# A quantised feed-forward is rebuilt with the weights in the expert loop, work by quarters and written-out pairs

## The chip, the core and the metric

The kernel runs on one core of a Trainium2 chip. A core has TensorE (PE in the profile), VectorE (DVE), ScalarE (ACT), GpSimd (POOL) and SyncE (SP), which only issues DMAs here. Each engine works through its own list of instructions in order, and the engines meet at semaphores. The metric is the time of one execution on the device in microseconds (us); smaller is better.

## The reference, cut to what matters

Two layers run on `x` of 16 x 256 tokens with 128 features. The first is relative-position attention and a mixture of 8 experts. The second is linear attention and a feed-forward whose operands are rounded to 4-bit floating point by blocks of 16. The change is about this last part:

```python
def fp4_quant_dequant(x):                      # blocks of 16 along the last dimension
    scale = jnp.maximum(jnp.max(jnp.abs(xb), axis=-1, keepdims=True) / 6.0, 1e-12)
    idx = jnp.searchsorted(_MID, jnp.abs(xb / scale))
    return _GRID[idx] * jnp.sign(xb / scale) * scale      # grid 0 .5 1 1.5 2 3 4 6
def fp4_linear(x, w):
    return einsum('bsk,nk->bsn', fp4_quant_dequant(x), fp4_quant_dequant(w))
h = layernorm(x) * (1 + cb) + sb
gate, up = fp4_linear(h, w_gate), fp4_linear(h, w_up)     # 352 hidden features
x = x + gb * fp4_linear(silu(gate) * up, w_down)
```

## The kernel before

The 4096 tokens are 32 tiles of 128 tokens (one token a partition). Four tiles are a chunk, eight tiles a quarter, two tiles a pair. `R2` holds the residual stream of all tiles.

**Expert loop** (about 556 to 831 us). Eight chunks `tc`, in each 16 half experts `k`. TensorE makes two products (`experts_up`, L1125 to L1127), ACT takes silu into `SG`, DVE multiplies (`hidden_product`, `hb_done`), ACT and DVE or POOL split the result into two half-precision parts (`low_hidden`, L608 on POOL), and TensorE makes the down product (`expert_down`), which DVE adds up (`weigh`). TensorE waits for the product two halves back (`hb_done`). Functions called `beside(tc, k)` put small pieces of other work at chosen places of this loop on each engine: the gating, and for some chunks statistics and normalisation of the next layer. Pieces are Python generators that give one instruction or a few at each `next`.

**Linear attention** (831 to 933 us). Its last step is eight output projections (L1233), each followed by a multiplication with the gate on DVE (`gate_projection`, L1528, semaphore `l_mul`) and an addition to `R2` on POOL (`residual`, L518, `l_od`).

**Preparation of the feed-forward** (933 to 998 us). DVE takes the statistics of the norm in two halves (L1306 to L1316). POOL clears `FN` (L637), SP loads the three weight matrices into it, POOL makes the inverse roots (`inverse_root`, L493), ACT centres the 32 tiles (`centre`, L712). DVE quantises the weights in two parts (L1779 to L1785, L1796; 768 and 352 columns), TensorE turns them (L1242, L1247), DVE copies them out of PSUM (L1800 to L1802). DVE scales the eight chunks (`scaled`, L1323), POOL adds the shift (`shifted`, L502). Then the input is quantised in four quarters, each 128x1024: seven DVE instructions (`quantise`), namely

```python
step(nc.vector.tensor_reduce(am[0], x, AX_X, ALU.max, apply_absolute_value=True))   # L1779
step(TS(am[2], am[0], ...))                # L1780, block scale
step(nc.vector.reciprocal(am[1], am[2]))   # L1781
step(STT(m, x, 2.0 ** -23 - 1.0, inv, ALU.mult, ALU.mult))                          # L1782
step(TS(s.bitcast(I32), m.bitcast(I32), ...))                                       # L1783
step(STT(m, s, 1.5 * 2 ** 22, m, ALU.max, ALU.add))                                 # L1784
return STT(m, s, 1.5 * 2 ** 22, m, ALU.max, ALU.subtract), scale                    # L1785
```

and on POOL the multiplication with the block scale (L644, into `XQ`). `step` waits for each instruction before the next. TensorE turns `XQ` (L959), ACT copies it to `R1` (L878).

**Pair loop** (998 to 1142 us). 16 pairs `m`, rolled in hardware loops (`Fori`) of two pairs on every engine:

- TensorE: `gate_and_up(m+1)` (L1261, 4 products of 352 columns from the stationary operand `XT`), then `hidden_and_down(m)`: six transposes of the quantised hidden `HQ` (L1270) and, after ACT's copy, six down products (L1277).
- ACT: `silu_gate` (L893, `SGP`, one buffer, 128x704), `evacuate_hidden` (L899, L900, `HT`, one buffer), `stationary` (L883, from `R1` to `XT`), `evacuate_output` (L889, `YB`).
- DVE, `hidden(m)`: the product `SGP` x up, up read from PSUM (L1825, `f_h`), and the seven steps of `quantise` on 128x704. The next gate product waits for `f_h`, since the up result lies in the bank that it writes.
- POOL: `scale_hidden` (L661, `f_q`), and `output`: multiplication with the gate (L651) and addition to `R2` (L655).
- SP: after every second pair 8 DMAs of finished tiles (L464).

Of the kernel before, what the change touches and what calls it, by code (L numbers as in the profile page):

```python
# [5 lines left out]

# [74 lines left out]
def adaln_program(nc, a, out):  # L81
# [17 lines left out]
    with outer:  # L99
# [74 lines left out]

        l1 = ExitStack()
# [18 lines left out]
        FN = sb("FN", [128, 6 * 128 + FF], F32, ff)  # L194
        WGU = sb("WGU", [128, 2, FF], F32, ff)
        WD1 = sb("WD1", [128, 3, 128], F32, ff)

        SGP = sb("SGP", [128, 2, FF], F32, ff)
        HQ = [sb(f"HQ{j}", [128, 2, FF], F32, ff) for j in range(2)]
        XT = [sb(f"XT{j}", [128, 2, 128], F32, ff) for j in range(2)]  # L200
        HT = sb("HT", [128, 2, 3, 128], F32, ff)
# [42 lines left out]
        f_ye, f_yg, x_round = sem("f_ye"), sem("f_yg"), sem("x_round")  # L244
# [36 lines left out]
        def _(sp):  # L281
# [170 lines left out]
            sp.wait_ge(l_od, 8)  # L452
# [8 lines left out]
            with sp.Fori(0, NT // 4) as c:  # L461
                sp.wait_ge(f_out, 2 * c + 2)
                for l in range(IL):
                    sp.dma_start(out_tok[l][:, bass.ds(4 * c, 4), :],  # L464
                                 R2[B * l:B * (l + 1), bass.ds(4 * c, 4), :]).then_inc(stored, 16)
# [4 lines left out]
        def _(gp):  # L470
# [17 lines left out]

            def inverse_root(n):
                for half in range(2):  # L490
                    tiles = slice(NT // 2 * half, NT // 2 * (half + 1))
                    gp.wait_ge(var_ready, 17 + half)
                    gp.tensor_tensor(LN[:, 2, tiles], LN[:, 1, tiles], LN[:, 5, tiles], ALU.pow).then_inc(root_done, 1)  # L493
                    gp.wait_ge(root_done, 17 + half)
                    gp.tensor_tensor(LN[:, 3, tiles], LN[:, 0, tiles], LN[:, 2, tiles], ALU.mult).then_inc(rstd_ready, 1)

            def shifted(order, dst, shift, ready):

                for c in range(8):
                    gp.wait_ge(scale_done, c + 1)  # L500
                    t = dst[:, 4 * c:4 * c + 4, :]
                    gp.tensor_tensor(t, t, shift.unsqueeze(1).to_broadcast([128, 4, D]), ALU.add).then_inc(ready, 1)  # L502
# [65 lines left out]
            for h in range(H - 1):  # L568
                sums_to_dram(h)
                normalise(h)  # L570
            for q in range(4):
# [63 lines left out]
            residual(l_mul, R2, [CT[j][:, :] for j in range(2)], l_od)  # L635
            gp.wait_ge(l_od, 8)
            gp.memset(FN[:, :], 0.0).then_inc(zeroed, 1)  # L637
            inverse_root(5)
            shifted(3, HN3, MOD[1][:, 3, :], pre_ready)
            BLOCKS = NT * D // 16 // 4  # L640
            for c in range(4):
                k = slice(BLOCKS * c, BLOCKS * (c + 1))
                gp.wait_ge(x_round, c + 1)
# [4 lines left out]
            def output(m, v):  # L648

                gp.wait_ge(f_ye, m + 2)  # L650
                gp.tensor_tensor(YB[v][:, :, :], YB[v][:, :, :], MOD[1][:, 5, :].unsqueeze(1).to_broadcast([128, 2, D]), ALU.mult)\  # L651
                    .then_inc(f_yg, 1)
                gp.wait_ge(f_yg, m + 1)
                x = R2[:, bass.ds(2 * m, 2), :]
                gp.tensor_tensor(x, x, YB[v][:, :, :], ALU.add).then_inc(f_out, 1)  # L655

            def scale_hidden(m, v):

                gp.wait_ge(f_round, m + 1)
# [3 lines left out]

            gp.sem_inc(f_q, 1)
            scale_hidden(0, 0)
            with gp.Fori(0, PAIRS // 2 - 1) as c:
                for v in range(2):
                    scale_hidden(2 * c + v + 1, 1 - v)
                    output(2 * c + v, v)
            scale_hidden(PAIRS - 1, 1)  # L670
            output(PAIRS - 2, 0)
            output(PAIRS - 1, 1)


        @block.scalar
        def _(act):
# [29 lines left out]

            def centre(k, src, dst, done, before=0):

                for n in range(NT):
                    if n % (NT // 2) == 0:  # L710
                        act.wait_ge(rstd_ready, 17 + n // (NT // 2))
                    last = A(dst[:, n, :], src[:, n, :], ACT.Identity, bias=LN[:, 3, n:n + 1], scale=LN[:, 2, n:n + 1])  # L712
                    if n % 4 == 3:
                        last.then_inc(done, 1)
# [94 lines left out]

            def high_hidden(tc, k):  # L810
# [62 lines left out]
            centre(5, R2, HN3, centred)  # L873

            def evacuate_x(chunks):
                for c in chunks:
                    act.wait_ge(t_done, 24 + c + 1)
                    A(R1[:, 512 * c:512 * c + 512], banks[4 + c % 2][:, :], ACT.Copy).then_inc(t_evac, 1)  # L878

            evacuate_x(range(6))  # L880

            def stationary(m, v):
                A(XT[v][:, :, :], R1[:, bass.ds(256 * m, 256)].rearrange("p (u t) -> p u t", u=2), ACT.Copy).then_inc(f_xt, 1)  # L883

            def evacuate_output(m, v):
                act.wait_ge(f_y, m + 2)
                if not (isinstance(m, int) and m < 2):
                    act.wait_ge(f_out, m - 1)
                A(YB[v][:, :, :], PS[:, 6:8, 0:128], ACT.Copy).then_inc(f_ye, 1)  # L889

            def silu_gate(m):
                act.wait_ge(f_gu, m + 1)
                A(SGP[:, :, :], gate_up[:, :, 0], ACT.Silu).then_inc(f_sg, 1)  # L893

            def evacuate_hidden(m):
                act.wait_ge(f_ht, m + 2)
                act.wait_ge(f_y, m + 1)
                t = PS[:, 4:6, 0:384].rearrange("p u (c t) -> p u c t", c=3)
                A(HT[:, :, 0:2, :], t[:, :, 0:2], ACT.Copy)  # L899
                A(HT[0:96, :, 2, :], t[0:96, :, 2], ACT.Copy).then_inc(f_hv, 1)  # L900

            act.sem_inc(f_hv, 1)
            act.sem_inc(f_ye, 1)
            act.wait_ge(t_evac, 30)
            stationary(0, 0)
            stationary(1, 1)
            silu_gate(0)
            evacuate_x(range(6, 8))
            act.wait_ge(t_evac, 32)
            stationary(2, 0)  # L910
            silu_gate(1)
            evacuate_hidden(0)
            stationary(3, 1)
            evacuate_output(0, 0)
            silu_gate(2)
            evacuate_hidden(1)
            stationary(4, 0)
            evacuate_output(1, 1)
            with act.Fori(1, PAIRS // 2 - 2) as c:
                for v in range(2):  # L920
                    silu_gate(2 * c + v + 1)
                    evacuate_hidden(2 * c + v)
                    stationary(2 * c + v + 3, 1 - v)
                    evacuate_output(2 * c + v, v)
            for m in range(PAIRS - 4, PAIRS):
                if m + 1 < PAIRS:
                    silu_gate(m + 1)
                evacuate_hidden(m)
                if m + 3 < PAIRS:
                    stationary(m + 3, (m + 1) % 2)  # L930
                evacuate_output(m, m % 2)
# [3 lines left out]
        def _(pe):  # L935
# [16 lines left out]
            def transposes(k, src, chunks=range(8)):  # L952

                for c in chunks:
                    pe.wait_ge(h_ready, 8 * k + c + 1)
                    if c >= 2:
                        pe.wait_ge(t_evac, 8 * k + c - 1)
                    for j in range(4):
                        last = tr(banks[4 + c % 2][:, 128 * j:128 * j + 128], src[:, 4 * c + j, :], ident)  # L959
                    last.then_inc(t_done, 1)  # L960
# [11 lines left out]
            for q in range(4):  # L972
                transposes(0, HN, (2 * q, 2 * q + 1))
# [128 lines left out]
            def linear_transposes(c):  # L1102
# [4 lines left out]
                elif c >= 2:  # L1107
                    pe.wait_ge(t_evac, 16 + c - 1)
                for j in range(4):
                    last = tr(banks[6 + c % 2][:, 128 * j:128 * j + 128], HN2[:, 4 * c + j, :], ident)  # L1110
                last.then_inc(t_done, 1)

# [34 lines left out]
            def beside(tc, k):  # L1147
# [90 lines left out]
            pe.wait_ge(f_w, 1)  # L1238
            for w in range(2):
                for c in range(3):  # L1240
                    m = (128, 128, 96)[c]
                    last = tr(banks[w][:, 128 * c:128 * c + m], FN[0:m, 384 * w + 128 * c:384 * w + 128 * c + 128],  # L1242
                              ident[0:m, 0:m])
            last.then_inc(f_tr, 1)
# [616 lines left out]
```

## Time and profile before

| | |
|---|---|
| time, median of 3 runs (lowest to highest) | 1143.52 us (1142.25 to 1144.01) |
| time of the profiled execution | 1143.78 us |
| span of its trace, first to last instruction | 1142.0 us |
| busy: TensorE, DVE, ACT, POOL | 884.3, 734.3, 453.7, 411.9 us |
| mean granted TensorE clock | 0.878 of full speed |
| first hidden maximum in the pair loop starts | 998.89 us |
| last instruction of the last rounding ends | 1127.10 us |

The device time is a little longer than the span of the trace. A granted clock of 1.00 is 2.4 GHz for TensorE and 0.50 is 1.2 GHz; a value between them is a mean over a stretch. Names with a "q" (SPq, POOLq) are an engine's queue of DMA issues. In a row, `out<-in` names the tiles, and what stands in square brackets is the idle time of the engine before the instruction and what ended it.

### The profile page before, as it was taken

What the parts mean: (1) busy time and instruction counts of PE and PEld (TensorE: products, weight loads), DVE (VectorE), ACT (ScalarE), POOL (GpSimd) and SP (SyncE); (2) the same over time, 40 slices, a digit from 0 to 9 for tenths busy, and PEclk for the clock granted to TensorE, in tenths of its full rate; (3) what the DMA queues carried; (4) which work ended last, traced back from release to release, by engine and by line L of the source; (5) the groups of instructions that cost most, each with busy time, mean ns of one, the idle gap of its engine ahead of it and who ended that gap; (6) DMA issues with size and microseconds to landing.
All of it is one profiled execution on the core that took longest, in us unless ns stands there. A gap on an engine that the chain in (4) does not pass through costs nothing.

```text
span 1142.0 us, 22164 instructions
## 1 busy us (share of the span) xinstructions
PE 884.3 (77%) x8587; PEld 671.1 (59%) x8587; DVE 734.3 (64%) x1571; ACT 453.7 (40%) x748; POOL 411.9 (36%) x447
## 2 busy tenths in 40 slices
PE   2484679999999999874689989999937850467774
PEld 1243668888888888653356656666615840254553
DVE  6683426555555655336687887888858768876664
ACT  4850123333333333245545565655633223222221
POOL 5552003333334333245223353334442056223232
PEclk8696889999999999896799999999978985578776
DMA  7075112233233323620000000000000000000000
GB/s 132 0 191 169 41 35 58 65 91 72 62 85 74 70 60 92 160 53 3 1 1 2 1 2 1 1 1 1 1 0 1 1 20 0 0 9 10 18 18 18
DMA packets 69608, 46.37 MB, mean 41 GB/s; under 512 B 35056, under 2 KB 60856, under 8 KB 68792
## 3 DMA queue, kind: packets, MB, share of 16 engines
q1 hardware_dynamic: 52776, 24.75, 9.7%
q0 software_dynamic: 8032, 19.11, 6.4%
q10 hardware_dynamic: 8704, 1.19, 0.6%
q8 instruction: 65, 1.06, 0.4%
q14 instruction: 31, 0.25, 0.1%
HBM read 30.05 MB, written 12.06 MB: 37 GB/s over the span
## 4 chain that ended last, share of the span: by engine, by line
PE 46%; DVE 23%; DMA 7%; POOL 7%; SPq 6%; ACT 5%; issue 5%; ACTq 0%; POOLq 0%; DVEq 0%
PE PS L1029 7%; PE PS L1125 5%; PE PS L1126 5%; PE PS L1127 5%; PE PS L1049 4%; PE PS L1009 3%; PE PS L1033 3%; PE PS L1010 3%; PE PS L1261 2%; SPq L336 2%; PE PS L1277 2%; DMA REG<-inverse_sums 2%; DVE HB L1682 2%; DVE REG L1479 2%; ACT REG L687 1%
## 5 line engine op out<-in xcount | busy, mean ns | idle before, releaser
L1460 DVE TENSOR_REDUCE MX<-PS 128x2 f32<-128x512 f32 x256 | 171.4, 686 | 172.2 <-PE PS L1010 170.6
L766 ACT ACTIVATE REG<-PS 128x1024 f32<-128x1024 f32 x128 | 131.5, 1027 | 242.2 <-PE PS L1033 239.4
L1029 PE MATMUL PS<-XX,TB 96*128 96x64 f16 x2048 | 160.0, 246 | 7.3 <-DMA XX<-NEG 4.5
L1009 PE MATMUL PS<-TM,YY 128*128 128x256 f16 x512 | 129.8, 285 | 32.8 <-DMA YY<-REG 15.2
L1029 PEld LDWEIGHTS PS<-XX,TB 96*128 96x128 f16 x2048 | 133.5, 120 | 22.8 <-issue 12.8
L608 POOL TENSOR_TENSOR HH<-HB,HH 128x512 f16<-128x512 f32 x64 | 75.6, 1181 | 171.2 <-ACT HH L813 171.2
L1010 PE MATMUL PS<-KM,YY 128*128 128x256 f16 x512 | 126.8, 279 | 0.0
L1682 DVE SCALAR_TENSOR_TENSOR HB<-PS,SG 128x512 f32<-128x512 f32 x128 | 87.5, 684 | 50.7 <-ACT SG L841 50.7
L841 ACT ACTIVATE SG<-PS 128x512 f32<-128x512 f32 x128 | 76.2, 595 | 110.3 <-PE PS L1127 110.0
L1033 PE MATMUL PS<-XX,KC 97*128 97x128 f16 x1024 | 107.8, 229 | 0.0
L1125 PE MATMUL PS<-XH,XX 128*128 128x512 f16 x256 | 98.8, 386 | 9.1 <-DVE HB L1682 8.9
L1126 PE MATMUL PS<-XH,XX 128*128 128x512 f16 x256 | 98.5, 385 | 0.0
L1127 PE MATMUL PS<-XH,XX 128*128 128x512 f16 x256 | 98.3, 384 | 0.0
L1009 PEld LDWEIGHTS PS<-TM,YY 128*128 128x128 f16 x512 | 73.7, 144 | 39.9 <-issue 15.3
L1125 PE MATMUL PS<-XX,HH 128*128 128x128 f16 x512 | 89.7, 220 | 7.8 <-issue 2.9
L1127 PE MATMUL PS<-XX,HH 128*128 128x128 f16 x512 | 89.9, 220 | 0.0
L1126 PE MATMUL PS<-XX,HH 128*128 128x128 f16 x512 | 89.8, 220 | 0.0
L813 ACT ACTIVATE HH<-HB 128x512 f16<-128x512 f32 x128 | 79.8, 623 | 8.0 <-DVE HB L1682 7.7
L1033 PEld LDWEIGHTS PS<-XX,KC 97*128 97x128 f16 x1024 | 76.4, 113 | 0.0
L1010 PEld LDWEIGHTS PS<-KM,YY 128*128 128x128 f16 x512 | 75.3, 147 | 0.7
L1049 PE MATMUL PS<-REG,V 128*32 128x256 f32 x1024 | 63.1, 388 | 1.1 <-ACT REG L766 1.1
L1674 DVE SCALAR_TENSOR_TENSOR ACC<-PS,CMBT,ACC 128x128 f32<-128x128 f32 x224 | 62.6, 342 | 1.5 <-PE PS L1127 1.3
(235 smaller groups left out, 1704.3 us busy)
## 6 DMA issues: line engine op xcount, KB each, us to landing
REG<-inverse_sums POOLq DMA_DIRECT2D x60, 128.0 KB, 2.9
YY<-queries_content ACTq DMA_DIRECT2D x224, 4.0 KB
KC<-keys_strips SPq DMA_DIRECT2D x16, 192.0 KB
keys_strips<-REG POOLq DMA_DIRECT2D x12, 224.0 KB, 8.0
R<-in_L_attn_x SPq DMA_DIRECT2D x32, 64.0 KB, 3.4
out<-R SPq DMA_DIRECT2D x64, 32.0 KB, 1.6
queries_position<-REG POOLq DMA_DIRECT2D x2, 960.0 KB, 12.9
queries_content<-REG POOLq DMA_DIRECT2D x2, 960.0 KB, 17.7
```

The costliest lines, as they stand in the source:

```text
L766: A(P[jt][:, 1024 * up:1024 * up + 1024].rearrange("p (k x) -> p k x", k=2), ST[u % 2], ACT.Exp).then_inc(exp_done, 1)
L813: A(HH[k % 4][:, 0, :], HB[k % 2][:, :], ACT.Copy).then_inc(hi_done, 1)
L1009: mm(o, yp[:, a], TM[p][:, 31 - a:31 - a + T], start=True, stop=False)
L1010: last = mm(o, yc[:, a], KM[p][:, :], start=False, stop=True)
L1029: mm(o_pos[:, a], TB[p][0:96, y0:y0 + 128], xp[0:96, 8 * bank + a], start=(a == 0), stop=False, skip_group_check=True)
L1033: last = mm(o[:, 128 * c:128 * c + 128].rearrange("p (b s a) -> p b s a", b=4, s=4), KC[p][0:97, c, 128 * jt:128 * jt + 128], xc[0:97, ban ...
L1049: last = mm(PV[32 * g:32 * g + 32, c, :].rearrange("p (q x) -> p q x", q=8), V[:, v0:v0 + 32], p[:, b], start=(jt == 0 and c % 2 == 0), st ...
L1125: mm(o, w[0], x[0], start=first, stop=False)
L1126: mm(o, w[0], x[1], start=False, stop=False)
L1127: return mm(o, w[1], x[0], start=False, stop=final)
L1460: nc.vector.tensor_reduce(MX[h % 2][:, 2 * kk:2 * kk + 2], banks[4 + kk % 2].rearrange("p (a j) -> p a j", a=2), AX_X, ALU.max)\
L1682: STT(HB[k % 2][:, :], banks[2 + k % 2], 1.0 / WS, SG[k % 2][:, :], ALU.mult, ALU.mult).then_inc(hb_done, 1)
```

## The change

The whole feed-forward is written anew; nothing before the expert loop changes except one memset.

1. **Weights in the expert loop.** `FN`, `WGU`, `WD1` and scratch now lie in `YY`. POOL clears `FN` after the last maximum product of the first attention (`max_mm`), SP loads the weights right after the first attention's last DMAs. DVE quantises them as 16 pieces: `beside` at chunk 1 from k = 6 on (10 pieces) and at chunk 3 from k = 10 on (6). TensorE turns them in chunk 4 at k = 2 (6 transposes) and k = 8 (3), ACT copies them out at k = 6 (one 128x704 instruction) and k = 10 (two).
2. **Quarters.** Statistics, root, centring, scaling and shifting go by quarter. DVE does the shift too (POOL's `shifted` is gone). POOL's order is residual 0, 1, 2, 3, root 0, residual 4, 5, root 1, residual 6, 7, roots 2, 3, `scale_input` 0 and 1, `product(0)`.
3. **DVE's order.** Gate 0 to 3, statistics 0, gate 4, 5, statistics 1, gate 6, 7; then norm 0, statistics 2, input 0, norm 1, statistics 3, input 1. The 22 pieces of norm 2, input 2, norm 3 and input 3 are taken one by one behind each step of the hidden quantising of the first pairs.
4. **Pairs written out.** No `Fori` on any engine, two buffers each for `SGP`, `UP`, `HT`; the input transposes go pair by pair into bank 7 and ACT copies from there to `XT`; `R1` is not used for them any more. The down product writes bank 6.
5. **The product moves.** ACT copies up into `UP` behind silu; POOL multiplies `SGP` x `UP`, both in SBUF. DVE keeps the seven steps.

```diff
             def hidden(m):
+                v = m % 2
+                if m == 1:
+                    ve.wait_ge(h_ready, 24 + 4)
+                ve.wait_ge(f_h, m + 1)
+                yield from quantised(HQ[v]..., *pair_buffers[v][0:2], pair_buffers[v][2:], hidden_step, f_round)
-                ve.wait_ge(f_sg, m + 1)
-                if not (isinstance(m, int) and m < 1):
-                    ve.wait_ge(f_q, m)
-                    ve.wait_ge(f_ht, m)
-                TT(HQ[v][:, :, :], SGP[:, :, :], gate_up[:, :, 1], ALU.mult).then_inc(f_h, 1)
...
+            for piece in (feed_norm(0), feed_statistics(2), feed_input(0), feed_norm(1), feed_statistics(3), feed_input(1)):
+                for _ in piece:
+                    pass
+            behind = itertools.chain(feed_norm(2), feed_input(2), feed_norm(3), feed_input(3))
+            for m in range(PAIRS):
+                for _ in hidden(m):
+                    next(behind, None)
...
+            def product(m):                                   # POOL
+                v = m % 2
+                gp.wait_ge(f_sg, m + 1)
+                if m >= 2:
+                    gp.wait_ge(f_ht, m - 1)
+                gp.tensor_tensor(HQ[v][:, :, :], SGP[v][:, :, :], UP[v][:, :, :], ALU.mult).then_inc(f_h, 1)
...
+            for m in range(PAIRS):                            # POOL, with scale_hidden and output as before
+                if m + 1 < PAIRS:
+                    product(m + 1)
+                scale_hidden(m)
+                if m in (2, 5):
+                    scale_input(2 + m // 5)
+                if m >= 3:
+                    output(m - 3)
...
+            def silu_gate(m):                                 # ACT
+                act.wait_ge(f_gu, m + 1)
+                if m >= 2:
+                    act.wait_ge(f_h, m - 1)
+                A(SGP[m % 2][:, :, :], gate_up[:, :, 0], ACT.Silu)
+                A(UP[m % 2][:, :, :], gate_up[:, :, 1], ACT.Copy).then_inc(f_sg, 1)
...
+            for m in range(PAIRS + 2):                        # ACT
+                if m + 1 < PAIRS:
+                    silu_gate(m + 1)
+                if 1 <= m <= PAIRS:
+                    evacuate_hidden(m - 1)
+                if m >= 2:
+                    evacuate_output(m - 2)
+                if m + 3 < PAIRS:
+                    stationary(m + 3)
...
+            def gate_and_up(m):                               # TensorE
+                pe.wait_ge(f_xt, m + 1)
+                if m:
+                    pe.wait_ge(f_sg, m)
...
+            for m in range(PAIRS + 2):                        # TensorE
+                if m + 1 < PAIRS:
+                    gate_and_up(m + 1)
+                if 1 <= m <= PAIRS:
+                    hidden_transposes(m - 1)
+                if m >= 2:
+                    down(m - 2)
+                if m + 3 < PAIRS:
+                    input_transposes(m + 3)
...
+                elif tc == 1 and k >= 6 or tc == 3 and k >= 10:     # DVE, beside the experts
+                    next(weights)
...
+                elif tc == 4 and k in (2, 8):                       # TensorE
+                    feed_transposes(k // 8)
...
+                elif tc == 4 and k in (6, 10):                      # ACT
+                    feed_weights(k // 4 - 1)
```

## Rows read from the trace of the kernel before

**Rows 1.** The page of the profile, its first line

```profile
span 1142.0 us, 22164 instructions
```

**Rows 2.** Busy time by stage: length, busy of PE PEld DVE ACT POOL, PEclk

```profile
933.00:998.00 65.00, 13.90 (x49) 10.11 (x49) 54.88 (x101) 18.82 (x43) 33.27 (x18) 0.53 0.03 8
...
1015.00:1032.00 17.00, 12.41 (x55) 9.33 (x56) 11.88 (x18) 4.67 (x11) 5.58 (x6) 0.80 0.08 15
```

**Rows 3.** The chain of waits, from 990 us: start, length, what

```profile
1020.04 1.39 POOL HQ L661
```

**Rows 4.** Timeline, 916 to 1000 us: start, length, instruction

```profile
926.82 0.69 DVE L1528 TENSOR_TENSOR CT<-PS,MOD 128x512 f32<-128x512 f32 x1 [0.20 <-PE PS L1233]
...
968.04 2.17 DVE L1784 SCALAR_TENSOR_TENSOR XX<-XX 128x1024 f32<-128x1024 f32 x1
...
977.15 1.22 DVE L1784 SCALAR_TENSOR_TENSOR XX<-XX 128x1024 f32<-128x1024 f32 x1
...
992.08 5.06 PE L1261 MATMUL PS<-WGU,XT 128*128 128x352 f32 x8 [1.13 <-ACT XT L883]
...
996.93 1.25 PE L959 MATMUL PS<-CON,XQ 128*128 128x128 f32 x8
...
998.89 0.89 DVE L1779 TENSOR_REDUCE AM<-HQ 128x44 f32<-128x704 f32 x1
```

**Rows 5.** Timeline of DVE in the pair loop, and its end

```profile
1014.12 0.89 DVE L1825 TENSOR_TENSOR HQ<-SGP,PS 128x704 f32<-128x704 f32 x1 [4.59 <-ACT SGP L893]
...
1015.05 0.89 DVE L1779 TENSOR_REDUCE AM<-HQ 128x44 f32<-128x704 f32 x1
...
1016.19 0.43 DVE L1781 RECIPROCAL AM<-AM 128x44 f32<-128x44 f32 x1
...
1019.07 0.89 DVE L1785 SCALAR_TENSOR_TENSOR XX<-XX 128x704 f32<-128x704 f32 x1
...
1126.21 0.89 DVE L1785 SCALAR_TENSOR_TENSOR XX<-XX 128x704 f32<-128x704 f32 x1
```

**Rows 6.** Busy time of TensorE in one busy stretch of a pair

```profile
1013.10:1018.95 5.85, 4.83 (x27) 1.00 0.00 0
```

**Rows 7.** Groups by line and shape, from 860 us: count, busy, mean ns

```profile
L661 POOL TENSOR_TENSOR HQ<-XX,AM 128x704 f32<-128x704 f32 x16 | 22.1, 1384 | 87.6 <-DVE XX L1785 87.6
...
L651 POOL TENSOR_TENSOR YB<-YB,MOD 128x256 f32<-128x256 f32 x16 | 11.6, 724 | 4.7 <-ACT YB L889 4.7
...
L518 POOL TENSOR_TENSOR R<-CT,R 128x512 f32<-128x512 f32 x8 | 9.9, 1269 | 61.8 <-DVE CT L1528 61.8
L644 POOL TENSOR_TENSOR XQ<-XX,AM 128x1024 f32<-128x1024 f32 x4 | 7.7, 1930 | 17.1 <-DVE XX L1785 17.1
...
L893 ACT ACTIVATE SGP<-PS 128x704 f32<-128x704 f32 x16 | 12.1, 757 | 40.9 <-PE PS L1261 40.9
```

**Rows 8.** Instructions of line 562: min/median/max ns

```profile
L562 POOL TENSOR_TENSOR REG<-REG x15: 2342/2365/2377, 190.3 to 501.0; 128x1024 f32<-128x1024 f32 x15
```

**Rows 9.** DVE's busy time, one quarter of statistics, one of quantising

```profile
841.30:844.10 2.80, 2.61 (x16) 0.56 0.00 0
979.50:986.80 7.30, 7.09 (x9) 0.50 0.00 0
```

**Rows 10.** Timeline, DVE and POOL beside each other, two stretches

```profile
955.12 5.25 POOL L502 TENSOR_TENSOR HN<-HN,MOD 128x512 f32<-128x512 f32 x1 [10.00 <-DVE HN L1323]
...
853.29 3.41 DVE L1361 TENSOR_TENSOR HN<-HN,MOD 128x512 f32<-128x512 f32 x2
```

**Rows 11.** Busy time, two expert chunks, and the weights' two parts

```profile
700.50:732.60 32.10, 31.61 (x290) 20.01 (x289) 25.95 (x72) 17.85 (x32) 12.00 (x12) 1.00 0.01 2
732.60:766.30 33.70, 32.78 (x298) 20.69 (x297) 26.80 (x62) 21.77 (x42) 14.34 (x14) 1.00 0.01 2
...
940.75:947.05 6.30, 6.03 (x9) 0.50 0.00 0
947.05:950.75 3.70, 3.44 (x8) 0.50 0.00 0
```

More of the change, by code:

```diff
@@ L7 @@
+import itertools
 from contextlib import ExitStack
@@ L570, in _ @@
                 normalise(h)
+            gp.wait_ge(max_mm, 16 * H)
+            gp.memset(FN, 0.0).then_inc(zeroed, 1)
             for q in range(4):
@@ L634, in _, with linear_residual, scale_input @@
             residual_bias(BO1, MOD[1][:, 2, :], R2, 3)
[L635 to L639, printed above, removed]
+            def linear_residual(c):
+                gp.wait_ge(l_mul, c + 1)
+                gp.tensor_tensor(R2[:, 4 * c:4 * c + 4, :], CT[c % 2][:, :].rearrange("p (n d) -> p n d", n=4),
+                                 R2[:, 4 * c:4 * c + 4, :], ALU.add).then_inc(l_od, 1)
             BLOCKS = NT * D // 16 // 4
-            for c in range(4):
-                k = slice(BLOCKS * c, BLOCKS * (c + 1))
-                gp.wait_ge(x_round, c + 1)
+            def scale_input(q):
+                k = slice(BLOCKS * q, BLOCKS * (q + 1))
+                gp.wait_ge(x_round, q + 1)
                 gp.tensor_tensor(XQ[:, :, :].rearrange("p n (k s) -> p (n k) s", s=16)[:, k],
@@ L662, in scale_hidden, with output @@
                                  pair_buffers[v][4].unsqueeze(2).to_broadcast([128, 2 * FF // 16, 16]), ALU.mult).then_inc(f_q, 1)
[L664 to L672, printed above, removed]
+            def output(m):
+                v = m % 2
+                gp.wait_ge(f_ye, m + 1)
+                gp.tensor_tensor(YB[v][:, :, :], YB[v][:, :, :], MOD[1][:, 5, :].unsqueeze(1).to_broadcast([128, 2, D]), ALU.mult)\
+                    .then_inc(f_yg, 1)
+                gp.wait_ge(f_yg, m + 1)
+                x = R2[:, 2 * m:2 * m + 2, :]
+                gp.tensor_tensor(x, x, YB[v][:, :, :], ALU.add).then_inc(f_out, 1)
+            for q in range(4):
+                linear_residual(2 * q)
+                linear_residual(2 * q + 1)
+                if q:
+                    quarter_root(5, q - 1)
+            quarter_root(5, 3)
+            scale_input(0)
+            scale_input(1)
+            product(0)
+            for m in range(PAIRS):
[6 more added lines that the diff above has]
+                    output(m - 3)
+            for m in range(PAIRS - 3, PAIRS):
+                output(m)
         @block.scalar
@@ L885, in evacuate_output, with stationary @@
[L885 to L889, printed above, removed]
+            def stationary(m):
+                v = m % 2
+                act.wait_ge(f_xtr, m + 1)
+                if m >= 2:
+                    act.wait_ge(f_gu, m - 1)
+                A(XT[v][:, :, :], banks[7][:, 0:256].rearrange("p (u t) -> p u t", u=2), ACT.Copy).then_inc(f_xt, 1)
@@ L914, in _ @@
[L914 to L925, printed above, removed]
+                v = m % 2
@@ L950, in _, with transposes @@
             tr(banks[7][:, 0:128], WN[:, 4, :], ident).then_inc(pe_prep, 1)
[L952 to L960, printed above, removed]
+            def transposes(c):
+                pe.wait_ge(h_ready, c + 1)
+                if c >= 2:
+                    pe.wait_ge(t_evac, c - 1)
+                for j in range(4):
+                    last = tr(banks[4 + c % 2][:, 128 * j:128 * j + 128], HN[:, 4 * c + j, :], ident)
+                last.then_inc(t_done, 1)
             def project(c):
@@ L972, in _ @@
             for q in range(4):
-                transposes(0, HN, (2 * q, 2 * q + 1))
+                transposes(2 * q)
+                transposes(2 * q + 1)
                 if q == 0:
@@ L1111, in linear_transposes, with feed_transposes @@
                 last.then_inc(t_done, 1)
+            def feed_transposes(part):
+                pe.wait_ge(f_w, part + 1)
+                if part == 0:
+                    pe.wait_ge(t_evac, 16 + 2)
+                    for w in range(2):
+                        for c in range(3):
+                            m = (128, 128, 96)[c]
+                            last = tr(banks[6 + w][:, 128 * c:128 * c + m], FN[0:m, 384 * w + 128 * c:384 * w + 128 * c + 128],
+                                      ident[0:m, 0:m])
+                else:
+                    pe.wait_ge(f_ev, 1)
+                    for c in range(3):
+                        m = (128, 128, 96)[c]
+                        last = tr(banks[6][0:m, 128 * c:128 * c + 128], FN[:, 768 + 128 * c:768 + 128 * c + m], ident)
+                last.then_inc(f_tr, 1)
             def logits(half):
@@ L1832, in _, with feed_statistics, feed_norm @@
-            hidden(0, 0, 0)
-            with ve.Fori(0, PAIRS // 2 - 1) as c:
-                for v in range(2):
-                    m = 2 * c + v
-                    hidden(m + 1, 1 - v, steps_hidden + m * steps_pair)
-            hidden(PAIRS - 1, 1, steps_hidden + (PAIRS - 2) * steps_pair)
+            def feed_statistics(q):
+                return quarter_statistics(q, l_od, 2 * q + 2)
+            def feed_norm(q):
+                return quarter_modulated(3, q, HN3, MOD[1][:, 4, :], MOD[1][:, 3, :], pre_ready)
@@ new lines, in feed_input, with hidden @@
+            def feed_input(q):
+                k = slice(BLOCKS * q, BLOCKS * (q + 1))
+                t = [QS[j][:, :].rearrange("p (k s) -> p k s", s=16)[:, k] for j in range(2)]
+                ve.wait_ge(pre_ready, 2 * q + 2)
+                yield from quantised(w[:, k], t[0], t[1], [AM[j][:, k] for j in range(3)], norm, x_round)
+            hidden_step = Later(ve, loop_dve)
+            def hidden(m):
+                v = m % 2
+                if m == 1:
+                    ve.wait_ge(h_ready, 24 + 4)
+                ve.wait_ge(f_h, m + 1)
+                yield from quantised(HQ[v][:, :, :].rearrange("p u (k s) -> p (u k) s", s=16), *pair_buffers[v][0:2],
+                                     pair_buffers[v][2:], hidden_step, f_round)
@@ new lines, in _ @@
+            for c in range(4):
+                linear_gate(c)
+            for _ in feed_statistics(0):
+                pass
+            for c in range(4, 6):
+                linear_gate(c)
+            for _ in feed_statistics(1):
+                pass
+            for c in range(6, 8):
+                linear_gate(c)
+            for piece in (feed_norm(0), feed_statistics(2), feed_input(0), feed_norm(1), feed_statistics(3), feed_input(1)):
+                for _ in piece:
+                    pass
```

252 lines of the change are left out of this document (100 added, 152 removed).

## The prediction, made before the changed kernel was run

> **What bounds the kernel now.** I read the busy time by stage first [rows 2]. From 933 to 998 us TensorE works 13.9 of 65 us and VectorE (DVE) 54.9: the feed-forward's preparation is a DVE stage with nothing beside it. In the pair loop (998 to 1127, 16 pairs) no engine is full: of 17 us, some two pairs, TensorE has 12.4, DVE 11.9, ACT 4.7, GpSimd (POOL) 5.6. The chain of waits says why [rows 3]: POOL's scaling, transposes, down product and the next gate product stand one behind the other. The gate product waits for `f_h`, the down product of the same pair stands ahead of it in TensorE's queue, and DVE idles 4.59 us before its product [rows 5]. The loop costs 1127.1 - 998.9 = 128.2 us from its first maximum (L1779) to the end of its last rounding (L1785) [rows 4, 5], 8.0 a pair. After it 14.9 us remain to the span's end at 1142.0 [rows 1, 5].
>
> **What the change takes from each engine.** In a pair DVE loses the product SGP x up (0.89 [rows 5]). Left are seven steps, 1015.05 to 1019.96 in the trace: 4.9 us with their waits [rows 5]. POOL gets that product, with both inputs in SBUF. The trace has no such 704-wide one; the nearest are 512 wide, 1.27 [rows 7], and 1024 wide, 2.37 [rows 8]: 2.15 ns an element, so 1.68 for 704. Bounds: 1.38, what its 704-wide scaling takes [rows 7], and 1.9. POOL then has 1.68 + 1.38 + 2 x 0.72 = 4.5 a pair. ACT gets a copy like its silu of the same form, 0.76 [rows 7], on top of 4.67 / 2 = 2.3 a pair [rows 2]: 3.1, cover enough. TensorE needs 4.83 a pair at 2.4 GHz [rows 6], and two input transposes (0.31, two of the eight in 1.25 [rows 4]): 5.1. With the orders written out, product m+1 stands ahead of scaling m, so by counts alone DVE and TensorE would set some 5.1.
>
> **But DVE and POOL get in each other's way.** A 512-wide POOL addition (1.27 in [rows 7]) took 5.25 while DVE's two-input products of L1323 ran in a stream [rows 10]; L1784 took 2.17 beside POOL and 1.22 alone [rows 4]. Two 512-wide DVE products beside POOL's additions took 3.41 [rows 10], so 1.70 for one of each: 0.69 (the width's price in [rows 4]) + 1.27 less 0.25, that is the sum of both durations less 0.12 at each handover. So I cost DVE's steps other than maximum and reciprocal, and all of POOL, as one resource. DVE's share is 4.9 less the maximum (0.89) and the reciprocal (0.43) and six gaps of 0.03: 3.4. A pair then has 4.5 + 3.4 = 7.9, less five to seven handovers (0.7): 7.2. This is above the 5.1 of TensorE and DVE, and it is the likeliest bound.
>
> **The loop afterwards.** Shared work between the first maximum and the last rounding: POOL 15 products 25.2, 15 scalings 20.8, twelve outputs 17.3 (the rest fall behind), two input scalings 3.9 [rows 7]; DVE 16 x 3.4 = 54.4, and of the deferred quarters 2 and 3, which now ride in the first three pairs, 2 x (4 x 0.69 + five steps of input quantising, 4.6 of the 7.3 us [rows 9]) = 14.6. Sum 136. Handovers give back 16 x 0.7 = 11, and some 2 us pass at semaphores: 127 us. So the loop gains nothing on its 128.2; bounds 123 (every handover saves) and 138 (none does).
>
> **The preparation.** DVE's path from the end of the fourth gate multiply, 926.82 + 0.69 = 927.5 [rows 4]: four quarters of statistics 4 x 2.7 [rows 9], four more gate multiplies 2.8, normalisation of quarters 0 and 1 (2 x 4 x 0.69 = 5.5, and 2 for POOL's residual additions beside it, between none and 4 x 1.0), two input quantisings 2 x 7.3 [rows 9], of which one waits for POOL's input scaling (1.5). Sum 37.2, to 964.7. Behind it, in POOL's order, the second input scaling 1.93 and the first product 1.68 [rows 7, 8], and I allow 1.5 for TensorE and ACT, since the first gate product is at half clock (5.06 with what interrupts it [rows 4]) and stands on the same moment: the first maximum at about 970, for 998.9 before: 29 earlier (25 to 33). Weights (9.5 us with the gaps, [rows 11]), their transposes and copies, two of four input quarters, half the normalisation and POOL's eight shifts (5.25 for the first [rows 10]) have left this stretch; the work that hides centring and roots is DVE's other quarters, and without that cover each quarter costs its 3 us of ACT.
>
> **The expert loop gets the weights.** Sixteen DVE pieces, 6.03 + 3.44 us [rows 11], nine transposes, three ACT copies. A chunk without normalisation takes 32.1 us, one with four 0.69 products and eight transposes 33.7 [rows 11]: 1.6 us for 2.8 of DVE work, TensorE being 31.6 busy of 32.1. At the same ratio 9.5 us cost 5.5; I take 5 (late next is `hb_done`, for which TensorE's next expert stands still). Bounds: 1, only the transposes, and 9.5. The memset and the five weight DMAs go to where SP and POOL have only the end of the attention behind them, far ahead of their use, at nothing; were they late, the first weights piece would hold DVE, and behind it every hidden product.
>
> **The tail.** As before 14.9, plus 1 because the down product of pair 14 now stands between the transposes and the down product of pair 15 (1.6 to 2.9, partly under the evacuation), less 0.5 since the last DMAs need no register arithmetic: 15.4 (14.5 to 17). The unrolled instructions I cost at nothing: their fetch lies beside the work; above zero I have no row for it.
>
> **Sum.** 970 + 127 + 15.4 + 5 = 1117.4 of span, against 1142.0. The profiled execution took 1143.78, 1.8 above its span and 0.26 above the median 1143.52. So 1119 us, 2.1% faster. Own range: 966 + 123 + 14.5 + 1 + 1.8 = 1106 to 974 + 132 + 16 + 8 + 1.8 = 1132.
>
> **Rivals.**
> *No handover saving.* If whole durations add, the loop is 138, 11 more: 1130. The 1.70 of the alternating products speaks against it, DVE's waits of up to a whole POOL instruction for it.
> The Trainium skill, "SBUF — State Buffer", "Who interferes with whom", says of a DVE instruction with two SBUF inputs beside a GpSimd one that reads SBUF that the later one "fully blocks"; by that rule it would be this 1130, and the trace agrees that they exclude each other (2.17 for 1.22), but not that nothing overlaps.
> *Little contention.* If POOL's instructions fall mostly under the maximum, the reciprocal and DVE's gaps, DVE is the bound: 16 x 5.0 + 20 for the deferred quarters = 100, 27 less: 1092. POOL's 4.5 of work against 1.3 us of such cover speaks against it.
> *TensorE stays at half clock.* The granted share was 0.80 in the loop [rows 2], falling behind idle stretches as in POOL's scaling. At 1.2 GHz a pair needs 2 x 4.83, and the input transposes, 9.8 (its short pauses stay). From the first gate product at about 962 to that of pair 15 TensorE's queue takes 15 x 9.8 = 147; then silu and copy 1.5, product 1.7, DVE 4.9: 1117, 20 after the forecast's 1097; with 2 more in the tail 1141. Against it: in its busy stretch the granted share was 1.00 [rows 6], and a pair has 2 us of slack to absorb slower stretches.
> *Slower: strict alternation of the two engines.* If POOL gets in only when DVE's chain of a pair is over, as in the 5.25 us row, product and scaling wait for the chain and the chain for the product: 4.9 + 4.5 + 0.2 = 9.6 a pair, 38 us more: 1157. It decides from 8.7 a pair (7.2 + 24.5/16). For it speaks that row; against it that L502 alternated one by one with DVE steps that wait on one another, as the loop's do.
>
> **Chances.** Forecast 0.56, no saving 0.14, little contention 0.11, half clock 0.11, alternation 0.08. Differences under 0.2% (2.3 us) can't be told from none in this kernel. The half-clock case lies on that line; so faster 0.86, same 0.04, slower 0.10. The range reaches from most of the way to the little-contention case up to the half-clock case: 1100 to 1141.
>
> **What would show it.** Right: first L1779-like maximum of the hidden at 970 plus 5; from pair 6 a period near 7.2 with the three-operand steps stretched (over 1.1 for 0.89) and POOL busy above 60%; TensorE idle over 1.5 us a pair; expert loop 5 us longer, most of it in chunk 1; tail 15.4. Wrong: a period of 5.2 (no shared resource), of 9.8 with a granted clock near 0.5, POOL instructions of 3 us and more, or chunks 1 and 3 longer by over 10 us together.

## The result and the profile after

The changed kernel takes 1113.29 us (median of 4 runs, 1111.39 to 1116.66) against 1143.22 for the kernel before in the same group of runs: ratio 0.9742, interval 0.9716 to 0.9767, 2.6% faster. The forecast was 1119, with a range of 1100 to 1141. The profiled execution is the slowest of the four: 1116.66 us with a span of 1114.9. Part of this scatter lies ahead of the changed code. The first hidden product of the expert loop starts between 553.0 and 558.2 us in the profiled executions of this study, though nothing but a memset was moved there. Below, lengths are therefore taken between instructions.

The page, first lines and the TensorE clock by slices (tenths of full speed; beside it stand [rows 1]):

```profile
span 1114.9 us, 21838 instructions
...
PE 870.3 (78%) x8587; PEld 663.7 (60%) x8587; DVE 750.3 (67%) x1573; ACT 461.1 (41%) x759; POOL 435.9 (39%) x459
...
PEclk7696789999999999987589999999996997689995
```

| stage | before | forecast | after |
|---|---|---|---|
| expert chunk 0 to chunk 7, starts of the first product | 242.7 | +5 | 245.6 (+3.0) |
| end of the fourth gate multiply to the first hidden maximum | 71.4 | 42.5 | 41.8 |
| first maximum to the end of the last rounding | 128.2 | 127 | 125.9 |
| steady period of a pair | 5.7 and 11.1 in turn | 7.2 | 7.08 |
| end of the last rounding to the span's end | 14.9 | 15.4 | 16.5 |

Of the 27.1 us by which the span fell, 26.3 are the earlier first maximum (972.57 for 998.89, the expert loop's 3 us already paid), 2.3 the loop, and the tail gives 1.6 back.

One steady pair in the timeline of the changed kernel (start, length, instruction; it answers to [rows 5], and the gate product at 1054.05 to [rows 6]):

```profile
1050.18 0.88 DVE L1392 TENSOR_REDUCE AM<-HQ 128x44 f32<-128x704 f32 x1
...
1050.34 1.39 POOL L654 TENSOR_TENSOR HQ<-XX,AM 128x704 f32<-128x704 f32 x1 [1.75 <-DVE XX L1410]
1051.09 0.68 DVE L1395 TENSOR_SCALAR AM<-AM 128x44 f32<-128x44 f32 x1
1051.68 0.73 POOL L661 TENSOR_TENSOR YB<-YB,MOD 128x256 f32<-128x256 f32 x1
...
1052.26 0.90 DVE L1401 SCALAR_TENSOR_TENSOR XX<-HQ,AM 128x704 f32<-128x704 f32 x1
...
1052.49 1.25 POOL L665 TENSOR_TENSOR R<-R,YB 128x256 f32<-128x256 f32 x1
...
1053.19 0.93 DVE L1404 TENSOR_SCALAR XX<-XX 128x704 int32<-128x704 int32 x1
1053.71 1.95 POOL L647 TENSOR_TENSOR HQ<-SGP,UP 128x704 f32<-128x704 f32 x1
...
1054.05 2.53 PE L1282 MATMUL PS<-YY,XT 128*128 128x352 f32 x8
1054.16 2.25 DVE L1407 SCALAR_TENSOR_TENSOR XX<-XX 128x704 f32<-128x704 f32 x1
...
1056.45 0.89 DVE L1410 SCALAR_TENSOR_TENSOR XX<-XX 128x704 f32<-128x704 f32 x1
...
1057.26 0.88 DVE L1392 TENSOR_REDUCE AM<-HQ 128x44 f32<-128x704 f32 x1
```

From maximum to maximum 1057.26 - 1050.18 = 7.08 us, DVE without a pause. But its instructions are stretched. L1407 starts 0.45 us after POOL's product and ends at 1056.41, 0.75 after the product's end: 2.25 us for work of 0.89. L1395 (0.19 alone) ends as POOL's scaling does, and L1404 (0.53 alone) takes 0.93 behind L665, which itself takes 1.25 for 0.72 behind L1401. It is a chain of turns, DVE, POOL, DVE, in which only the maximum (0.88) and the reciprocal (0.43) run beside POOL undisturbed. The groups of both engines over the whole feed-forward (count, busy, mean ns, idle before; they answer to [rows 7]):

```profile
L1407 DVE SCALAR_TENSOR_TENSOR XX<-XX 128x704 f32<-128x704 f32 x16 | 28.2, 1762 | 0.4
...
L1410 DVE SCALAR_TENSOR_TENSOR XX<-XX 128x704 f32<-128x704 f32 x16 | 15.6, 975 | 0.4
```

```profile
L647 POOL TENSOR_TENSOR HQ<-SGP,UP 128x704 f32<-128x704 f32 x16 | 30.6, 1914 | 7.9 <-ACT UP L903 4.4 <-PE PS L1293 3.5
L654 POOL TENSOR_TENSOR HQ<-XX,AM 128x704 f32<-128x704 f32 x16 | 23.4, 1465 | 40.1 <-DVE XX L1410 40.1
L665 POOL TENSOR_TENSOR R<-R,YB 128x256 f32<-128x256 f32 x16 | 17.6, 1098 | 1.3
L661 POOL TENSOR_TENSOR YB<-YB,MOD 128x256 f32<-128x256 f32 x16 | 12.3, 769 | 3.6 <-ACT YB L921 3.6
```

L1407 and L1410 are the same form and take 0.89 alone. One carries nearly all of the wait (mean 1762 ns), the other little (975). The product's 1914 ns is its 1.67 plus a wait. In the same windows as [rows 2] and [rows 11], the second busy column being TensorE's loads, then DVE, ACT, POOL and the granted clock:

```profile
1048.50:1062.70 14.20, 9.65 (x58) 7.25 (x57) 13.79 (x15) 5.86 (x12) 10.54 (x9) 1.00 0.10 19
598.20:632.70 34.50, 33.07 (x325) 21.10 (x324) 29.93 (x69) 18.75 (x34) 11.81 (x12) 1.00 0.01 1
...
702.60:735.60 33.00, 32.36 (x297) 20.73 (x296) 26.01 (x72) 18.92 (x35) 11.63 (x12) 1.00 0.01 1
```

In the steady pairs DVE is busy 13.8 of 14.2 us, POOL 10.5, TensorE 9.65 at a granted clock of 1.00. The two chunk rows, the one with the weights' first ten pieces and the one with their transposes, each stand some 1 us over the same chunk before (33.4 and 32.2).

### The profile page after: what moved, and what is told of

The parts are those of the page before. It is cut to its first block, busy times and chain, and to the rows that moved or that the text cites. A ratio compares the mean times of both kernels' runs of the same rounds, so it can differ in the third digit from the quotient of the medians.

```text
span 1114.9 us, 21838 instructions
## 1 busy us (share of the span) xinstructions
PE 870.3 (78%) x8587; PEld 663.7 (60%) x8587; DVE 750.3 (67%) x1573; ACT 461.1 (41%) x759; POOL 435.9 (39%) x459
## 4 chain that ended last, share of the span: by engine, by line
PE 44%; DVE 29%; SPq 6%; DMA 6%; ACT 5%; issue 5%; POOL 4%; ACTq 0%; POOLq 0%; DVEq 0%
PE PS L1036 8%; PE PS L1151 5%; PE PS L1153 5%; PE PS L1152 5%; PE PS L1056 5%; PE PS L1016 4%; PE PS L1040 4%; PE PS L1017 4%; DVE XX L1407 3%; SPq L339 2%; DVE XX L1401 2%; DVE HB L1741 2%; DVE XX L1410 2%; DVE REG L1536 2%; DVE AM L1392 1%
## 5 line engine op out<-in xcount | busy, mean ns | idle before, releaser
L770 ACT ACTIVATE REG<-PS 128x1024 f32<-128x1024 f32 x128 | 131.5, 1027 | 242.8 <-PE PS L1040 239.1
L856 ACT ACTIVATE SG<-PS 128x512 f32<-128x512 f32 x128 | 76.2, 595 | 112.2 <-PE PS L1153 112.0
L1151 PE MATMUL PS<-XX,HH 128*128 128x128 f16 x512 | 90.9, 221 | 7.3 <-issue 2.9
L1153 PE MATMUL PS<-XX,HH 128*128 128x128 f16 x512 | 91.2, 222 | 0.0
L1152 PE MATMUL PS<-XX,HH 128*128 128x128 f16 x512 | 91.1, 222 | 0.0
```

The source lines that it names most:

```text
L770: A(P[jt][:, 1024 * up:1024 * up + 1024].rearrange("p (k x) -> p k x", k=2), ST[u % 2], ACT.Exp).then_inc(exp_done, 1)
L1151: mm(o, w[0], x[0], start=first, stop=False)
L1152: mm(o, w[0], x[1], start=False, stop=False)
L1153: return mm(o, w[1], x[0], start=False, stop=final)
```

## Experiments

The times are medians; the ratios are to the kernel before, which took 1143.04, 1141.68 and 1142.16 us beside the three groups of runs (E1 to E4; E5 to E8; E9 and E5's second). Each diff is against the changed kernel.

**E1, POOL makes every product twice.** The first goes to a scratch tile that nothing reads.

```diff
+                gp.tensor_tensor(TW[v][:, :, :], SGP[v][:, :, :], UP[v][:, :, :], ALU.mult).then_inc(f_tw, 1)
                 gp.tensor_tensor(HQ[v][:, :, :], SGP[v][:, :, :], UP[v][:, :, :], ALU.mult).then_inc(f_h, 1)
```

> GpSimd makes every hidden product a second time into a scratch tile (1.67 us more a pair on GpSimd, nothing more on the other engines; the scratch is not used). Shared-resource theory (DVE's two-input and fast steps and all of GpSimd take turns): period 7.08 + 1.67 - 0.12 = 8.6 us, 15 pairs, so 23 us slower than the changed kernel's 1113: 1136 us. Rival (DVE's own chain of a pair sets the period, GpSimd has about 2.5 us idle a pair in which the second product hides): period stays 7.1, 1113 to 1116 us.

Measured: 1137.7 us, ratio 0.995 (0.9927 to 0.9973); steady period 8.43. POOL has 2.5 us idle a pair (40.1 over 16 before L654 above), yet a product of 1.67 costs 1.35. Both products' groups in E1, 1030 to 1120 us:

```profile
L651 POOL TENSOR_TENSOR HQ<-SGP,UP 128x704 f32<-128x704 f32 x10 | 23.1, 2314 | 0.0
L650 POOL TENSOR_TENSOR TW<-SGP,UP 128x704 f32<-128x704 f32 x10 | 19.9, 1989 | 0.0
```

They take 2314 and 1989 ns for 1.67 us of work, each with a wait for DVE. POOL's idle time is not free time: while it waits for the last rounding, DVE holds what it needs.

**E2, the product back on DVE, up read from PSUM**, and **E3, on DVE with ACT's copy of up in SBUF.** In both, POOL has no product. In E2 ACT makes no copy, and the gate product waits for `f_h` as in the kernel before; in E3 both stay as in the changed kernel. PSUM is where TensorE's results land, SBUF where all other tiles lie.

```diff
             def hidden(m):
-                if m == 1:
-                    ve.wait_ge(h_ready, 24 + 4)
+                if m < 2:
+                    ve.wait_ge(h_ready, 24 + 2 * m + 2)
+                ve.wait_ge(f_sg, m + 1)
+                if m >= 2:
+                    ve.wait_ge(f_ht, m - 1)
+                TT(HQ[v][:, :, :], SGP[v][:, :, :], gate_up[:, :, 1], ALU.mult).then_inc(f_h, 1)   # E3: UP[v]
                 ve.wait_ge(f_h, m + 1)
```

> The product goes back to DVE, which reads up from PSUM (one SBUF input); GpSimd loses it, ACT loses its copy, the next gate product waits for DVE's product. Everything else as in the changed kernel. Shared-resource theory: shared work 3.4 + 2.83 less handovers is 5.6, so DVE's own 4.9 + 0.9 plus some waits for GpSimd sets about 6.2: 13 us faster than the changed kernel, 1099 to 1102 us. Rival (DVE is simply full, each pair's time is its instructions): 0.9 us more a pair, period 8.0, 1127 us.

> As the run before (product on DVE), but DVE reads ACT's copy of up, so both inputs lie in SBUF; DVE's instruction costs the same alone (0.89). Shared-resource theory: 3.4 + 0.89 + 2.83 = 7.1 less 0.6 for handovers, 6.4 to 6.6 a pair, some 4 to 6 us slower than with up from PSUM: 1104 to 1107 us. Rival (the place of an input makes no difference): the same time as the run before within 2 us.

Measured: E2 1099.99 us, ratio 0.9606 (0.9573 to 0.964), period 6.11. E3 1107.26 us, ratio 0.9669 (0.9639 to 0.9699), period 6.31. In E2, DVE's product, maximum and the two steps that wait for POOL, then POOL's scaling:

```profile
1046.94 0.88 DVE L1856 TENSOR_TENSOR HQ<-SGP,PS 128x704 f32<-128x704 f32 x1
1047.86 0.89 DVE L1388 TENSOR_REDUCE AM<-HQ 128x44 f32<-128x704 f32 x1
1048.78 0.43 DVE L1391 TENSOR_SCALAR AM<-AM 128x44 f32<-128x44 f32 x1
...
1049.71 1.01 DVE L1397 SCALAR_TENSOR_TENSOR XX<-HQ,AM 128x704 f32<-128x704 f32 x1
...
1047.10 1.39 POOL L654 TENSOR_TENSOR HQ<-XX,AM 128x704 f32<-128x704 f32 x1 [3.24 <-DVE XX L1406]
```

and the same in E3:

```profile
1055.77 0.93 DVE L1401 TENSOR_SCALAR XX<-XX 128x704 int32<-128x704 int32 x1
...
1058.48 0.88 DVE L1857 TENSOR_TENSOR HQ<-SGP,UP 128x704 f32<-128x704 f32 x1
...
1060.32 0.33 DVE L1392 TENSOR_SCALAR AM<-AM 128x44 f32<-128x44 f32 x1
...
1058.64 1.97 POOL L654 TENSOR_TENSOR HQ<-XX,AM 128x704 f32<-128x704 f32 x1 [2.32 <-DVE XX L1407]
```

DVE's product takes 0.88 in both. POOL's scaling, which starts 0.16 after it in both, takes 1.39 where up comes from PSUM and 1.97 where both inputs lie in SBUF. So giving DVE 0.89 us more a pair made a pair 0.97 shorter, and the place of one input is worth 0.2 a pair and 4.4 in the loop (116.4 for 112.0). ACT's copy, which E3 keeps, isn't the cause: DVE works without a pause in E3's pair, and the 0.2 stand in its waits for POOL (0.14 and 0.40 in the two steps shown, for 0.24 and 0.12 in E2). The other 3 of the 7 us between the two medians aren't shown to come from the input. In the profiled executions E3 began its expert loop 2.4 us later, ahead of any difference in code, and its last down product ran at a granted clock of 0.50 for 1.00 in E2 (2.92 for 1.59 us).

**E4, the output's gate multiply on DVE from PSUM; E5, this and E2 together.** POOL's multiply (L661) and ACT's evacuation of the output (L921) go.

```diff
+            def gate_output(m):
+                ve.wait_ge(f_y, m + 1)
+                if m >= 2:
+                    ve.wait_ge(f_out, m - 1)
+                TT(YB[m % 2][:, :, :], banks[6][:, 0:256].rearrange("p (u d) -> p u d", u=2), ..., ALU.mult).then_inc(f_yg, 1)
             for m in range(PAIRS):
-                for _ in hidden(m):
+                for k, _ in enumerate(hidden(m)):
+                    if k == 0 and m >= 3:
+                        gate_output(m - 3)
                     next(behind, None)
```

> The multiplication of the output with the gate moves from GpSimd to DVE, which reads the down product from PSUM (0.42 us, one SBUF input), and ACT's evacuation of it goes. Shared-resource theory: 0.72 less of shared work a pair, 0.42 more of DVE work that GpSimd doesn't feel: period 6.5, 13 outputs, so 8 us and about 1 in the tail: 1104 us. Rival (DVE is full): 0.42 more a pair, 1119 us.

> Both moves at once: product on DVE with up from PSUM, and the output's multiplication with the gate on DVE from PSUM. Shared-resource theory with DVE's own chain as the next bound: with the product alone a pair took 6.11, of which DVE's own instructions are 5.9; 0.42 more makes 6.4 a pair, 4 to 5 us more in the loop, about 1 less in the tail: 1102 to 1105 us, so worse than the product alone (1100). Rival (the two gains, 13 and 8 us, are independent and add): 1092 us.

> The two moves to DVE together, once more beside the silu order, for comparison on the same chip: 1098.6 us within 0.2%. And as a second look at how far the start of the expert loop differs between executions of unchanged code ahead of it (552 to 558 us so far).

Measured: E4 1105.69 us, ratio 0.9665 (0.9631 to 0.9699), period 6.68. E5 1098.57, ratio 0.9621 (0.9608 to 0.9634), and again 1098.01, ratio 0.9616 (0.96 to 0.9633), period 6.00. The single moves gain 13 and 8 us, together 15: the independent sum (1092) is refuted. So are my 6.4 for the period and the 1102 to 1105 us that followed from it: I added 0.42 to E2's 6.11 and left out that E2's DVE still waited for POOL (L1391 0.43 for 0.19, L1397 1.01 for 0.89). In E5 POOL has 0.72 less a pair, and the step that took 1.01 takes 0.89. Busy time in E5, DVE's being the third number pair:

```profile
1020.00:1080.00 60.00, 46.15 (x269) 36.05 (x268) 57.97 (x90) 17.62 (x37) 22.67 (x21) 0.98 0.11 21
```

DVE is busy 57.97 of 60 us: now its own instructions are the period. E5 can't be told from E2 by its time (the intervals of their ratios overlap).

**E6, no deferral: quarters 2 and 3 before the loop.** POOL's input scalings 2 and 3 move with them, and ACT's last centring goes ahead of `stationary(0)`.

```diff
-            for piece in (..., feed_norm(1), feed_statistics(3), feed_input(1)):
+            for piece in (..., feed_norm(1), feed_statistics(3), feed_input(1), feed_norm(2), feed_input(2), feed_norm(3), feed_input(3)):
```

> The changed kernel with input quarters 2 and 3 normalised and quantised before the pair loop instead of piecewise in its first pairs. By the trace of the changed kernel the first eight pairs cost 14 us over their later period; before the loop the 22 pieces would cost DVE 2 x (2.8 + 7.3) = 20, and the last input scaling stands before the first product in either case: 5 to 8 us slower, 1119 to 1122 us. Rival (the shared work is the same wherever it stands, so its place is of no account): 1113 us.

Measured: 1118.14 us, ratio 0.9797 (0.9781 to 0.9813), 5 us slower than the changed kernel. The loop falls from 125.9 to 109.0, and the first maximum comes at 992.13, 19.6 later. The chain of waits there is DVE's, ending in one scaling and the product:

```profile
977.55 2.95 DVE HN L1378 x2
...
988.54 1.93 POOL XQ L637
990.47 1.64 POOL HQ L647
992.13 0.90 DVE AM L1389
```

**E7, the weights behind the linear attention**, that is, out of the expert loop; transposes and copies follow there.

```diff
-                elif tc == 1 and k >= 6 or tc == 3 and k >= 10:
-                    next(weights)
...
             for c in range(6, 8):
                 linear_gate(c)
+            for _ in weights:
+                pass
```

> The changed kernel with the weights' quantising, transposes and copies taken out of the expert loop and put behind the last gate multiply of the linear attention. DVE's path there grows by 9.7 us (the before kernel took 9.7 for them), the expert loop becomes 3 us shorter (chunk 7 starts 3.0 us later in the changed kernel than before, TensorE being nearly full there): 6 to 8 us slower, 1119 to 1121 us. Rival (in the preparation they would hide behind roots and centring, which are waited for anyway): 1110 us.

Measured: 1122.16 us, ratio 0.982 (0.9803 to 0.9838). Chunk 0 to chunk 7 takes 242.8 again, so pieces and transposes cost 2.8 to 3.0 there. From the first gate multiply to the first maximum it is 55.1 us for 46.4: 8.8 more, where the weights' instructions take DVE 11.4 (939.15 to 950.58). At 1122.16 the time is 1 us above the range expected.

**E8, E2 with seven deferred pieces taken before the first hidden.** Just ahead of the loop over the pairs, `next(behind)` is called seven times.

> Product on DVE with up from PSUM, and seven of the 22 deferred pieces (4.7 us of DVE work) taken before the first hidden quantising, where DVE idles 5.7 us in the changed kernel's trace behind the second input quarter. If that idle time is free, the loop's first pairs lose these pieces: 3 to 5 us faster than 1100, 1095 to 1097 us. Rival (the first pairs are bound by something else than DVE and shared work, or the pieces delay the second input scaling on GpSimd and with it the first product): 1100 us or more.

Measured: 1100.34 us, ratio 0.963 (0.9614 to 0.9647), no gain. The loop is 3.1 us shorter than E2's, the first maximum 2.8 later after the first gate multiply. The timeline of DVE and POOL before it:

```profile
967.26 3.02 DVE L1377 TENSOR_TENSOR HN<-HN,MOD 128x512 f32<-128x512 f32 x2
...
973.61 0.83 DVE L1856 TENSOR_TENSOR HQ<-SGP,PS 128x704 f32<-128x704 f32 x1
...
967.49 2.25 POOL L637 TENSOR_TENSOR XQ<-XX,AM 128x1024 f32<-128x1024 f32 x1 [4.47 <-DVE XX L1406]
```

Two products of 0.69 took 3.02 beside POOL's second input scaling, and the hidden product, for which silu was ready at 970.61, began at 973.61. The rival's second half holds the other way round: the pieces delayed DVE by 3 us and POOL's scaling by 0.3 (2.25 for 1.93).

**E9, E5 with the first silu ahead of centring the last quarter on ACT.**

> The two moves to DVE together, and ACT takes the first silu before it centres the last quarter. In the changed kernel's chain of waits the last centring (3.07 us) and the table load (1.25) stand ahead of the first silu, which began 969.38, while the first gate product began at 964.15. If that chain sets the first hidden maximum, it comes 1 to 2 us earlier relative to the first gate multiply and the time falls by as much, 1097 us. Rival (the first gate product at half clock or DVE's second input quarter sets it, and centring the last quarter later delays the deferred pieces): no change from 1098.6 us, or slower.

Measured: 1096.56 us, ratio 0.9587 (0.957 to 0.9604). From the first gate multiply to the first maximum 45.2 us, and 45.3 in the second run of E5: nothing gained. The chain of waits shows the rival's reason, a gate product at half clock (granted 0.51 there), with silu right behind:

```profile
966.26 4.70 PE PS L1265 x8
...
970.98 0.77 ACT SGP L896
```

Its median lies 1.5 us under that of E5's second group, but its profiled execution is slower (spans 1099.2 and 1097.4, the expert loop beginning 1.9 us later), and no later stretch of the trace is shorter by more than 0.1. I don't call it a gain. E5 and E9 are the fastest versions, 1.3 to 1.5% under the changed kernel and 3.8 to 4.1% under the kernel before.

## Why the prediction was right, point by point

**Mechanism: the one resource of DVE and POOL.** Right. The period is 7.08 for 7.2. E1 lengthens it by work put on the engine with idle time, E2 shortens it by work given to the engine without, E3 isolates the second SBUF input. One sign came out otherwise: the three-operand steps were to take over 1.1 us each, but L1401 and L1410 take 0.90 and 0.89, and L1407 alone 2.25.

**Size of a handover.** The 0.12 was taken from two alternating products. In the steady pair L1407 ends 0.75 after the product for 0.89, that is 0.14; in E1 1.67 more work costs 1.35 with two more handovers, 0.16 each. The rival without saving (7.9 a pair, 1130 us) is refuted.
The Trainium skill, "SBUF — State Buffer", "Who interferes with whom", has a DVE instruction with two SBUF inputs contend with a GpSimd one that reads SBUF, and one with at most one SBUF input not; of the later one it says that it "fully blocks", and by that rule a pair is 7.9. The traces agree on which of the two products contends (E2's leaves the scaling at 1.39, E3's makes it 1.97), and differ by these 0.12 to 0.16 us at each turn.

**The product's price.** 1.68 by the slope between 512 and 1024 columns; the first, undisturbed one took 1.67. Right.

**The preparation.** 42.5 forecast, 41.8 measured. In the chain of waits before the first maximum ACT's centring of the last quarter and the table load stand ahead of silu:

```profile
964.99 3.07 ACT HN L800 x8
...
968.08 1.25 ACT L902
...
969.38 0.76 ACT SGP L902
970.13 0.66 ACT UP L903
...
970.86 1.68 POOL HQ L647
...
972.57 0.89 DVE AM L1392
```

The forecast had the second input scaling and the product on the path, and the last centring hidden. Here the product waited 1.9 us for ACT after POOL's scaling had ended (968.95). By E9 ACT's order isn't the whole cause: with silu first, the half-clock gate product ends at the same time. The allowance of 1.5 stood for these 1.9, and DVE's path to the end of the second quantising was 1.1 shorter than added up (36.1 for 37.2), so the two errors partly cancel.

**The expert loop.** The term that was mis-sized: 5 forecast, 3.0 measured (E7 gives it back: 242.8). Taking all of the 1.6 us of a normalising chunk for its DVE work failed: in [rows 11] TensorE's busy time differs by 1.17 us between the two chunks, with the eight transposes, and DVE's by only 0.85, not 2.8. The trace after has +1.2 in chunk 1, +0.5 and +0.4 in the next two, +0.8 in chunk 4. Chunk 4 has TensorE's nine transposes and ACT's copies but no piece of DVE, so about 0.8 goes with them and about 2.1 with DVE's pieces; no run moved one without the other. That most of the loss would be in chunk 1 did not come true.

**Deferral.** Costed as shared work in the loop (18.5 of 136) and no DVE time before it. E6 shows 16.9 in the loop against 19.6 ahead of it. By the medians deferral is worth 5 us, a point that the prediction didn't state; the two stretches account for 2.7 of them, and where the rest lies isn't shown.

**The tail.** 16.5 for 15.4. The down product of pair 14 stands between as forecast, but at half clock (granted 0.50), and the last one then waits for ACT to empty the bank that both share:

```profile
1098.52 1.39 POOL HQ L654
...
1099.96 1.54 PE PS L1293 x6
1101.50 2.57 PE PS L1304 x12
...
1104.62 2.92 PE PS L1304 x12
```

From the end of the last rounding to the last down product's start it is 6.2 us, 4.0 before. The DMAs' part is 5.3 for 5.9, as forecast. The length itself depends on the execution: E7 has the same code there, its two last down products took 2.12 and 1.59 us for 2.57 and 2.92 (granted 0.65 and 1.00 for 0.50 twice), and its tail is 14.7. So the 1.1 over the forecast is the clock of this one execution and not work that the forecast left out.

**The other rivals.** Little contention (1092) and half clock (1141) are refuted by the period and by a granted clock of 1.00 in it; slow stretches stay in the first pairs (granted 0.73 from 995 to 1010 us) and in the tail. Alternation (1157) is refuted too: no POOL instruction in the loop took 3 us (the longest 2.91). That POOL gets in because each of DVE's steps waits for the one before fits this, but no run tests it.

**What the forecast missed in sum.** 1119 against 1113.3: 2.0 us too much for the expert loop, 0.7 for the preparation and 1.1 for the loop, 1.1 too little for the tail and 0.3 elsewhere, so 2.5 in the profiled execution (span 1114.9 for 1117.4). The other 3 are that this execution was the slowest of four.

**What the parts of the change are worth.** The forecast judged them together. Part 1 (weights) is worth 9 us by E7, deferral 5 by E6, and part 5 costs 13: E2 is the changed kernel with the product given back to DVE. E2 divides the product as the kernel before does, and takes 6.11 us a pair where that took 8.4 in the mean; this comes with the written-out order, the second buffers and the new banks of part 4, which no run takes apart.

## What to carry to other kernels

Before work goes from DVE to an idle GpSimd, add DVE's steps with two SBUF inputs and its fast scalar steps (here L1395 and L1404) to all of GpSimd's. If that sum (here 7.9 a pair, less some 0.14 at each turn) is above either engine's own, it is the likely period, and GpSimd's idle time is no room. An operand left in PSUM takes a DVE instruction out of that sum; here this was worth more than the copy that frees the bank early (E2 and E3). Gains found one by one stop adding as soon as the next bound, here DVE's own chain, is reached.

## What the runs showed of the hardware that was not expected

The wait falls on one step of a row of like ones: in the steady pair L1407 takes 2.25 us and L1410, of the same form and right behind, 0.89. So a long mean on one line needn't mean that this line is dear. And 0.89 us a pair of further work on DVE, which had no pause, shortened the kernel by 13 us (E2).
